# A fused Mamba and local-attention kernel: other group sizes, small steps moved from VectorE to GpSimd, joined VectorE operations, and products of zeros ahead of the first group's matmuls

## The chip, the cores and the metric

The kernel runs as one program on one core of a Trainium2 chip. The metric is device time in microseconds of that core. The time of a kernel is the median of its runs. Beside the timed runs there is one execution under the hardware profiler, and all rows below come from it.

## The reference, cut to what matters

The input is 16 sequences of 256 tokens with 128 features, all in float32. The work is a Mamba-like block, a transformer of two layers, and a normalisation after each of the two.

```python
# Mamba block, for x of shape (16, 256, 128)
u = silu(causal_conv4(x @ in_w + in_b))                    # 256 channels
delta = softplus((u @ dt1_w + dt1_b) @ dt2_w + dt2_b)
A = -exp(A_log)                                            # 16 states
h[t] = exp(delta*A) * h[t-1] + (exp(delta*A) - 1)/A * B * u   # a scan over 256 tokens
y = (sum_n C[n]*h[n] + D*u) * silu(x @ gate_w + gate_b)
x = layernorm(x + y @ out_w + out_b)
# two layers of local attention and a gated FFN
for l in 0, 1:
    q, k, v = split(shift_token(x) @ wqkv[l])              # 8 heads of 64
    q, k = rotary(l2norm(q)*qs), rotary(l2norm(k)*ks)      # windows of 64, own and previous
    x = x + softmax(8*q@k.T, masked) @ v @ wo[l]
    a, g = split(layernorm(shift_token(x)) @ w1[l] + b1[l])   # 341 hidden
    x = x + (a * gelu(g)) @ w2[l] + b2[l]
out = layernorm(x)
```

`shift_token` takes the second half of the features from the token before.

## The kernel before, in words

The sequences are cut into groups (`SIZES`). Before the change there are eight groups of two sequences, each 512 tokens or four tiles of 128. A group goes through the Mamba block on its own, then through attention and FFN of layer 0, then of layer 1. `QUAD` lists the (layer, group) pairs in the order in which attention and FFN take them, and `TILE` numbers the 64 (layer, group, tile) triples q = 0 to 63. Steps of Mamba take a group number `g`, steps of attention a tile number `q`, steps of the FFN a pair number `f`.

Each engine runs one written list of steps (`PE_ORDER`, `ACT_ORDER`, `DVE_ORDER`, `POOL_ORDER`, `SP_ORDER`). An engine never takes a later step first: when a step waits for a semaphore, all behind it on that engine waits too. So Mamba of group g+1, attention of layer 0 and of layer 1 are interleaved by the lists, not by the hardware.

- Mamba: `u_in` multiplies with `in_w` (TensorE), `convolve` makes the four-tap convolution (VectorE), `silu_u` and `silu_gate` follow (ScalarE), `rank` and `step_in` are the two small products for the step size, `softplus` is Abs, Exp and Ln on ScalarE, and `step_size` adds on VectorE. Then come 16 times one `decay` (ScalarE, Exp) and one `scan` (VectorE, all channels and sequences of the group in one instruction), whose result `state_y` sums on TensorE in the PSUM banks `Y`. `gated`, `mamba_out`, `mamba_sum` and `mamba_norm` end the block. All products of this block share the banks `Y`, so group g+1's `u_in` waits for group g's `gated`.
- Attention of a tile: `qk_in` and `v_in`; `squares` (ScalarE), `sums` (VectorE), `scale` (GpSimd, the power of -0.5) make the inverse norms `rn`; `rope` (VectorE) and `rotate` (GpSimd, for the keys) the rotation; `qk_T` transposes, `scores` multiplies; `row_max` (VectorE) takes the maximum and, before the change, also the product `nbias`; `softmax` (ScalarE) waits for `nbias`; then `probs_T`, `weighted`, `attended`, `out_T`.
- FFN of a pair: `attn_out`, `attn_sum`, `shift` (TensorE, the shifted half of the features), `ffn_stats`, `ffn_rstd` (GpSimd), `ffn_norm`, `norm_T`, `up_gate`, `gelus`, `up_a`, `hidden`, `down`, `ffn_sum`. All its products but the first two of `up_gate` pass through the one PSUM bank `M`.

A table of functions is loaded on ScalarE wherever the next function isn't in the table that is loaded (`ACT_TABLE_LOAD` in the profile). The diagonal matrices `diag` of `state_y` and the rotation tables are made at the start on GpSimd. Every matmul in float32 shows as two records in the trace.

Of the kernel before, what the change touches and what calls it, by code (L numbers as in the profile page):

```python
# [88 lines left out]
state_y 1 8, state_y 1 9, out_T 2, state_y 1 10, probs_T 3, state_y 1 11, weighted 3, state_y 1 12, out_T 3,
attn_out 0, state_y 1 13, state_y 1 14, state_y 1 15, shift 0, mamba_out 1, u_in 2, norm_T 0, layer_T 0 1,  # L90
up_gate 0, gate_in 2, qk_in 4, up_a 0 0, v_in 4, rank 2, qk_in 5, step_in 2, up_a 0 1, qk_T 4, up_a 0 2, qk_in 6,
v_in 5, scores 4, qk_in 7, down 0, qk_T 5, layer_T 1 0, probs_T 4, v_in 6, skip 2, scores 5, state_y 2 0,
state_y 2 1, weighted 4, state_y 2 2, state_y 2 3, probs_T 5, out_T 4, qk_T 6, v_in 7, scores 6, state_y 2 4,
weighted 5, state_y 2 5, qk_in 8, out_T 5, probs_T 6, v_in 8, state_y 2 6, qk_T 7, scores 7, qk_in 9,
state_y 2 7, weighted 6, state_y 2 8, out_T 6, probs_T 7, v_in 9, qk_T 8, state_y 2 9, weighted 7, scores 8,
out_T 7, qk_in 10, state_y 2 10, v_in 10, state_y 2 11, attn_out 1, probs_T 8, state_y 2 12, state_y 2 13,
qk_T 9, state_y 2 14, scores 9, qk_in 11, state_y 2 15, weighted 8, shift 1, mamba_out 2, probs_T 9, out_T 8,
u_in 3, qk_T 10, v_in 11, norm_T 1, scores 10, layer_T 0 2, gate_in 3, weighted 9, up_gate 1, probs_T 10,
up_a 1 0, qk_T 11, out_T 9, qk_in 12, scores 11, v_in 12, rank 3, weighted 10, up_a 1 1, qk_in 13, out_T 10,
probs_T 11, v_in 13, step_in 3, up_a 1 2, weighted 11, qk_T 12, qk_in 14, down 1, scores 12, layer_T 1 1,  # L100
out_T 11, qk_in 15, attn_out 2, qk_T 13, v_in 14, probs_T 12, shift 2, scores 13, skip 3, state_y 3 0,
weighted 12, out_T 12, norm_T 2, state_y 3 1, probs_T 13, v_in 15, state_y 3 2, qk_T 14, up_gate 2, weighted 13,
scores 14, state_y 3 3, up_a 2 0, state_y 3 4, out_T 13, up_a 2 1, qk_in 16, up_a 2 2, probs_T 14, state_y 3 5,
# [1426 lines left out]
```

## Time and profile before

| | us |
|---|---|
| median of 3 runs | 1129.08 (1127.99 to 1129.78) |
| the profiled execution's own time | 1122.38 |
| its span, first to last instruction | 1120.6 |
| TensorE busy with matmuls | 959.9 |
| VectorE busy | 917.7 |
| ScalarE busy | 821.5 |
| GpSimd busy | 479.2 |
| mean granted clock of TensorE | 0.943 of 2.4 GHz |

The span is what the rows cover; the execution's own time is 1.8 us longer. Busy time is a sum over stages that differ: the first 143 us and the last 110 us hold most of TensorE's idle time. The end of a matmul in the trace is modelled, so start-to-start distances say more than durations.

### The profile page before, as it was taken

The page shows a single profiled execution, that of the slowest core. Times are in us where ns is not written, and L with a number is a line of the kernel's source. Part 1 is how long each engine was busy: PE and PEld are TensorE (multiplying, and loading weights), DVE is VectorE, ACT ScalarE, POOL GpSimd, SP SyncE. Part 2 cuts the span into 40 slices and gives each one's busy share as a digit, 9 for nine tenths or more (in the row PEclk, how much of TensorE's full clock was granted, in tenths as well). Part 3 has the DMA queues.
Part 4 walks back from the last instruction along what each step waited for, and adds up shares of the span by engine and source line. Part 5 has one row for each costly group of instructions (what it writes and reads, how often), then busy time and mean ns, then how long its engine had stood idle before and what let it go on. Part 6 is the DMA issues. An engine that isn't in the chain of part 4 may idle for free. (4 is left out here: it accounts for less than half of the span.)

```text
span 1120.6 us, 26559 instructions
## 1 busy us (share of the span) xinstructions
PE 959.9 (86%) x10304; PEld 562.4 (50%) x10304; DVE 917.7 (82%) x1628; ACT 821.5 (73%) x1835; POOL 479.2 (43%) x308
## 2 busy tenths in 40 slices
PE   4466788789999999999989999999999899985865
PEld 1022443446464655556465556465555656753552
DVE  4787897899889998999889999999899966753822
ACT  3527765886998779886989689887997678772731
POOL 2704501653354444563345436535447354521701
PEclk8589888999999999999999999999999999998976
DMA  7000100100100001000000101010100001000100
GB/s 233 0 1 15 25 2 2 28 16 11 30 16 11 17 15 35 25 16 19 21 6 16 35 16 35 11 35 6 35 16 16 16 12 29 21 11 5 35 1 20
DMA packets 22000, 25.54 MB, mean 23 GB/s; under 512 B 2614, under 2 KB 13937, under 8 KB 21873
## 3 DMA queue, kind: packets, MB, share of 16 engines
q1 hardware_dynamic: 21873, 23.82, 8.1%
q8 instruction: 82, 1.34, 0.5%
q14 instruction: 45, 0.37, 0.1%
HBM read 9.13 MB, written 2.10 MB: 10 GB/s over the span
## 5 line engine op out<-in xcount | busy, mean ns | idle before, releaser
L718 POOL TENSOR_TENSOR rn<-ssc,expo 128x16 f32<-128x16 f32 x64 | 214.3, 3349 | 415.9 <-DVE ssc L1057 358.3
L993 DVE TENSOR_TENSOR_SCAN scan<-du,decay 128x1028 f32<-128x1028 f32 x128 | 292.6, 2319 | 1.8 <-ACT decay L804 1.8
L859 ACT ACTIVATE prob<-BB,nbias,rn 128x128 f32<-128x128 f32 x464 | 205.1, 465 | 26.9 <-DVE nbias L1100 25.6
L804 ACT ACTIVATE decay<-delta,negA 128x1024 f32<-128x1024 f32 x128 | 144.5, 1155 | 22.6 <-DVE scan L993 22.4
L1197 PE MATMUL YY<-scan,diag 64*64 64x512 f32 x1024 | 146.5, 658 | 16.7 <-DVE scan L993 16.4
L1197 PE MATMUL A<-wqkv,hT 128*128 128x512 f32 x256 | 125.1, 611 | 8.4 <-DVE ks L1076 5.9
L724 POOL TENSOR_TENSOR kr<-kc,ks 128x512 f32<-128x512 f32 x64 | 93.1, 1455 | 27.0 <-DVE ks L1076 25.4
L859 ACT ACTIVATION_READ_ACCUMULATOR prob<-BB,nbias,rn 128x1 f32 x464 | 98.8, 213 | 0.0
L1053 DVE TENSOR_REDUCE ss<-sq 128x16 f32<-128x1024 f32 x64 | 77.3, 1208 | 22.4 <-ACT sq L822 22.4
L822 ACT ACTIVATE sq<-A 128x512 f32<-128x512 f32 x128 | 72.3, 605 | 28.4 <-PE A L1197 25.9
L1096 DVE TENSOR_REDUCE nmax<-BB 128x4 f32<-128x512 f32 x116 | 74.4, 683 | 20.2 <-PE BB L1197 19.5
L1197 PEld LDWEIGHTS C<-v_even,probT 128*64 128x64 f32 x1024 | 65.8, 140 | 45.4 <-issue 40.1
L847 ACT ACTIVATE qkT<-BB 128x512 f32<-128x512 f32 x116 | 63.0, 598 | 32.3 <-PE BB L1349 32.0
L1197 PE MATMUL C<-v_even,probT 128*64 128x64 f32 x1024 | 74.5, 227 | 7.4 <-ACT v_odd L838 5.9
L1197 PE MATMUL M<-hnT,w 128*85 128x512 f32 (+1 forms) x128 | 70.4, 632 | 10.7 <-ACT hid L885 8.0
L828 ACT ACTIVATE probT<-BB 128x1024 f32<-128x1024 f32 x58 | 59.8, 1031 | 23.9 <-PE BB L1331 23.5
L1197 PE MATMUL C<-wqkv,hT 128*128 128x512 f32 x128 | 71.5, 640 | 6.7 <-ACT oT L869 3.2
L1197 PEld LDWEIGHTS A<-wqkv,hT 128*128 128x128 f32 x256 | 45.2, 191 | 61.9 <-issue 61.0
L1197 PE MATMUL C<-v_odd,probT 128*64 128x64 f32 x1024 | 74.9, 228 | 0.0
L727 POOL TENSOR_TENSOR kr<-kr,rn 128x512 f32<-128x512 f32 x64 | 71.0, 1109 | 5.0
L1197 PEld LDWEIGHTS M<-wo,oT 128*128 128x128 f32 x512 | 61.2, 198 | 14.3 <-ACT oT L869 7.9
L1197 PE MATMUL M<-wo,oT 128*128 128x128 f32 x512 | 63.4, 284 | 5.0 <-ACT oT L869 3.6
(159 smaller groups left out, 1942.7 us busy)
## 6 DMA issues: line engine op xcount, KB each, us to landing
v_even<-v_odd SPq DMA_DIRECT2D x96, 128.0 KB, 2.4
xT<-in_xT SPq DMA_DIRECT2D x8, 256.0 KB, 3.1
x<-in_x SPq DMA_DIRECT2D x8, 256.0 KB, 3.9
out<-outb SPq DMA_DIRECT2D x8, 256.0 KB, 2.4
wqkv<-in_wqkv SPq DMA_DIRECT2D x1, 1536.0 KB
w<-in_w SPq DMA_DIRECT2D x1, 682.0 KB
wo<-in_wo SPq DMA_DIRECT2D x1, 512.0 KB
bv<-in_bv SPq DMA_DIRECT2D x1, 328.0 KB
```

Of the source, the lines that this page charges most:

```text
L718: pool.tensor_tensor(rn[:, q % 2, :], ssc[:, :], expo[:, 0:2 * HEADS], ALU.pow).then_inc(rn_sb, 1)
L724: pool.tensor_tensor(kr[:, :], kc[:, :], ks[:, :], ALU.add).then_inc(rope_add, 1)
L727: pool.tensor_tensor(heads(kr[:, :]), heads(kr[:, :]), rn[:, q % 2, HEADS:].unsqueeze(2).to_broadcast((P, HEADS, DH)), ALU.mult).then_inc( ...
L804: act.activation(decay[:, at % A_RING, both(g), 1:], delta[:, both(g), :], ACT.Exp, scale=negA[:, n:n + 1]).then_inc(decay_sb, 1)
L822: act.activation(sq[:, a, :], A[a][:, :], ACT.Square).then_inc(sq_sb, 1)
L828: act.activation(probT[:, :, :, :].rearrange("p w h x -> p (w h x)"), pair(q)[:, :], ACT.Copy).then_inc(pT_sb, 1)
L847: act.activation(qkT[:, :, :, lo:lo + WIN], bank_of(q, r)[:, :].rearrange("p (a c x) -> p a c x", a=2, c=PAIRS), ACT.Copy).then_inc(qkT_sb, 1)
L859: ins = act.activation(prob[:, h, :], bank_of(q, a)[:, c * P:(c + 1) * P], ACT.Exp, bias=nbias[:, q % 2, h:h + 1], scale=rn[:, q % 2, h:h ...
L993: dve.tensor_tensor_scan(state, step, a, 0.0, ALU.add, ALU.mult).then_inc(scan_sb, 1)
L1053: dve.tensor_reduce(ss[:, :], sq[:, :, :].rearrange("p a (h x) -> p (a h) x", x=DH), AX.X, ALU.add).then_inc(ss_sb, 1)
L1096: dve.tensor_reduce(nmax[:, q % 2, a::2], bank_of(q, a)[:, :].rearrange("p (c x) -> p c x", x=P), AX.X, ALU.max, negate=True).then_inc(max ...
L1197: return pe.matmul(dst, lhsT, rhs, start=start, stop=stop, skip_group_check=True)
```

## The change

1. `SIZES` becomes ten groups: one sequence each in the first two and the last two, two in the six between. `QUAD` and all five lists are new. `part_a`, `part_b` and the rarely taken `scan_general` are cut to fit.
2. `softplus` loads one table that holds both Exp and Ln (set number 6). An Exp on a single element ahead of everything loads the first table.
3. From VectorE to GpSimd move the maximum with 1e-24 (`ssc`, now in `scale`), the product `nbias` (a step of its own, `exp_bias`) and the addition of eps in three norms (`rstd`).
4. VectorE's `rope` takes q and k in two operations in place of four, `row_max` both banks in one in place of two; `attended` loses its reciprocal to a step `inverse`, which the list puts earlier. Two more buffers let steps run ahead (`qkc`, `qks`, `rden`), and x3 has three in place of two.
5. `shift` also copies the unshifted half of the features into PSUM, by a product with the identity, so that `ffn_stats` and `ffn_norm` handle 128 columns at once.
6. At the start the loads are divided over SP's queue and ScalarE's, with semaphores of their own; `diag` is made by 2 GpSimd operations in place of 34; the rotation tables are made on VectorE.
7. `keep_busy(n)` issues n products of zeros (128x128 by 128 columns) on TensorE in the first group: 18 before `u_in`, 4 before `gate_in`, 14 before `rank`, 4 before `step_in`, 14 before `skip`.

```diff
-SIZES = (2, 2, 2, 2, 2, 2, 2, 2)
+SIZES = (1, 1, 2, 2, 2, 2, 2, 2, 1, 1)
+X3_RING = 3
...
+QUAD = [(0, 0), (0, 1), (0, 2), (1, 0), (1, 1), (0, 3), (1, 2), (0, 4), (1, 3), (0, 5), (1, 4), (0, 6), (1, 5),
+        (0, 7), (1, 6), (0, 8), (0, 9), (1, 7), (1, 8), (1, 9)]
...
 def scale(q):
+    pool.wait_ge(ss_sb, q + 1)
+    pool.tensor_scalar(ssc[:, :], ss[:, :], 1e-24, None, ALU.max).then_inc(ssc_sb, 1)
...
+def exp_bias(q):
+    pool.wait_ge(rn_sb, q + 1)
+    pool.wait_ge(max_sb, q + 1)
+    pool.tensor_tensor(nbias[:, q % 2, :], nmax[:, q % 2, :], rn[:, q % 2, 0:HEADS], ALU.mult).then_inc(nmax_sb, 1)
...
-def rstd(dst, ve, g, done):
+def rstd(dst, mv, ve, g, nth, aggr, var, done):
     n = tiles_of(g)
+    pool.wait_ge(aggr, nth)
+    pool.tensor_scalar(ve[:, 0:n], mv[:, 0:n, 1], EPS, None, ALU.add).then_inc(var, 1)
+    pool.wait_ge(var, nth)
     pool.tensor_tensor(dst[:, 0:n], ve[:, 0:n], expo[:, 0:n], ALU.pow).then_inc(done, 1)
...
-    for n in range(0, NST + 1):
-        ins = pool.tensor_scalar(diag[:, h, n, :], ident64[:, :], wsum[:, h, n:n + 1], None, ALU.mult)
+    ins = pool.tensor_tensor(diag[:, h], ident64[:, :].unsqueeze(1).to_broadcast(blocks),
+                             wsum[:, h, :].unsqueeze(2).to_broadcast(blocks), ALU.mult)
...
 def softplus(g):
+    load_table(EXP_AND_LN)
...
 def rope(q):
-    for a in range(2):
-        dve.tensor_tensor(heads(dst_c), heads(A[a][:, :]), cos, ALU.mult)
-        dve.tensor_tensor(dst_s..., swap, sin, ALU.mult).then_inc(rope_mul, 1)
+    dve.tensor_tensor(dst_c, src, cos, ALU.mult)
+    dve.tensor_tensor(dst_s, src[:, :, :, ::-1, :], sin, ALU.mult).then_inc(rope_mul, 2)
...
 def row_max(q):
-    for a in range(2):
-        dve.tensor_reduce(nmax[:, q % 2, a::2], bank_of(q, a)..., AX.X, ALU.max, negate=True).then_inc(max_sb, 1)
-    dve.tensor_tensor(nbias[:, q % 2, :], nmax[:, q % 2, :], rn[:, q % 2, 0:HEADS], ALU.mult).then_inc(nmax_sb, 1)
+    dve.tensor_reduce(nmax[:, q % 2, :]..., pair(q)..., AX.X, ALU.max, negate=True).then_inc(max_sb, 1)
...
 def ffn_stats(f):
     for i in range(tiles_of(g)):
-        dve.bn_stats(f_st[:, i, 0, :], x2[:, i, 0:D // 2])
-        ins = dve.bn_stats(f_st[:, i, 1, :], late[:, i, :])
+        ins = dve.bn_stats(f_st[:, i, :], rows[:, i, :])
...
+def keep_busy(n):
+    for _ in range(n):
+        mm(BB[:, 0:P], zeros[:, :], zeros[:, :])
...
 def shifted(f):
     for i in range(tiles_of(g)):
-        dst = M[:, i * D // 2:(i + 1) * D // 2]
-        ins = mm(dst, shift[:, :], x2[:, i, D // 2:], True, i % 2 == 0)
+        lo, mid, hi = i * D, i * D + D // 2, (i + 1) * D
+        mm(M[:, lo:mid], ident[:, :], x2[:, i, 0:D // 2])
+        ins = mm(M[:, mid:hi], shift[:, :], x2[:, i, D // 2:], True, i % 2 == 0)
```

In the new lists the first group's Mamba runs alone, then the second's; the first tile's `qk_in` stands between their products, but VectorE's list has no attention step until the second group's 16 scans are done (`gated 1, mamba_sum 1, sums 0, conv0 2, conv1 2, rope 0, ...`). The end of TensorE's list is `... weighted 63, up_a 18 0, up_a 18 1, out_T 63, up_a 18 2, down 18, attn_out 19, shift 19, norm_T 19, up_gate 19, up_a 19 0, up_a 19 1, up_a 19 2, down 19`; before it was `... weighted 63, out_T 63, attn_out 15, shift 15, ... down 15`.

## Rows read from the trace of the kernel before

**Rows 1.** The page: busy time, share of the span and instructions.
```profile
PE 959.9 (86%) x10304; PEld 562.4 (50%) x10304; DVE 917.7 (82%) x1628; ACT 821.5 (73%) x1835; POOL 479.2 (43%) x308
```

**Rows 2.** Stretches of the span: start:end, length, busy us by engine, clock, DMA.
```profile
0.00:36.00 36.00, 13.11 (x16) 3.44 (x16) 13.94 (x37) 15.05 (x17) 15.03 (x39) 0.74 0.55 181
36.00:76.00 40.00, 26.07 (x128) 4.25 (x128) 39.67 (x16) 17.20 (x16) 13.71 (x15) 0.68 0.00 1
76.00:110.00 34.00, 24.97 (x128) 11.75 (x128) 22.91 (x45) 19.82 (x27) 12.59 (x8) 0.90 0.04 13
...
143.00:950.00 807.00, 746.23 (x8352) 443.02 (x8350) 727.47 (x1281) 656.01 (x1479) 369.85 (x206) 0.99 0.08 19
...
1008.00:1079.00 71.00, 49.96 (x561) 32.29 (x560) 36.24 (x96) 37.53 (x100) 25.25 (x16) 0.90 0.07 16
1079.00:1121.00 42.00, 23.05 (x88) 16.20 (x86) 10.99 (x45) 4.49 (x6) 5.53 (x5) 0.70 0.05 13
```

**Rows 3.** Waits of TensorE from 143 to 950 us, those that VectorE ended: total, times, longest.
```profile
PE C L1394 <- DVE o_s L1088: 6.2, 7, 2.5
...
PE M L1423 <- DVE hn L1141: 5.1, 5, 2.3
...
PE A L1197 <- DVE ks L1076: 3.9, 5, 2.2
...
PE YY L1197 <- DVE scan L993: 3.4, 4, 1.3
```

**Rows 4.** Groups by line: operands, shapes, count, busy us, mean ns, idle before.
```profile
L993 DVE TENSOR_TENSOR_SCAN scan<-du,decay 128x1028 f32<-128x1028 f32 x128 | 292.6, 2319 | 1.8 <-ACT decay L804 1.8
...
L1141 DVE TENSOR_SCALAR hn<-M,f_mv,f_rs 128x64 f32<-128x64 f32 x64 | 21.6, 338 | 0.0
...
L885 ACT ACT_TABLE_LOAD x16 | 20.5, 1283 | 6.8 <-PE A L1197 6.6
...
L1197 PE MATMUL M<-x,shift 128*128 128x64 f32 x128 | 20.1, 280 | 0.9 <-DVE x L1113 0.9
...
L1057 DVE TENSOR_SCALAR ssc<-ss 128x16 f32<-128x16 f32 x64 | 16.8, 262 | 4.5 <-POOL rn L718 2.4
...
L1123 DVE BATCH_NORM_STATS2 f_st<-M 128x6 f32<-128x64 f32 x64 | 13.8, 215 | 0.3 <-issue 0.3
...
L1100 DVE TENSOR_TENSOR nbias<-nmax,rn 128x8 f32<-128x8 f32 x64 | 12.6, 197 | 6.7
```

**Rows 5.** Timeline of the start: start us, us, engine, line, operation, what ended the idle.
```profile
2.40 1.76 DVE L910 MEMSET v_even<- 128x2048 f32 x1 [0.38 <-issue]
...
6.04 3.78 PE L1197 MATMUL YY<-xT,in_w 128*128 128x512 f32 x4 [6.04 <-DMA gate_w<-in_gate_w]
...
11.96 1.98 PE L1197 MATMUL YY<-xT,gate_w 128*128 128x512 f32 x4 [2.14 <-ACT upre L762]
...
27.63 1.28 ACT L793 ACT_TABLE_LOAD   x1
28.92 1.06 ACT L793 ACTIVATE th<-th 128x1024 f32<-128x1024 f32 x1
...
36.29 39.67 DVE L993 TENSOR_TENSOR_SCAN scan<-du,decay 128x1028 f32<-128x1028 f32 x16 [1.48 <-ACT decay L804]
```

**Rows 6.** Timeline of TensorE in the last FFN.
```profile
1080.48 6.34 PE L1197 MATMUL M<-wo,oT 128*128 128x128 f32 x32 [0.69 <-ACT oT L869]
...
1096.44 3.43 PE L1197 MATMUL A<-hnT,w 128*128 128x512 f32 x4 [0.96 <-ACT hnT L876]
...
1108.13 5.27 PE L1197 MATMUL M<-w,hid 128*128 128x128 f32 x24 [0.93 <-DVE hid L1150]
```

**Rows 7.** Timeline of GpSimd's power and VectorE's scans around 342 us.
```profile
341.79 4.83 POOL L718 TENSOR_TENSOR rn<-ssc,expo 128x16 f32<-128x16 f32 x1 [1.99 <-DVE ssc L1057]
...
395.76 2.91 POOL L718 TENSOR_TENSOR rn<-ssc,expo 128x16 f32<-128x16 f32 x1 [15.38 <-DVE ssc L1057]
...
341.62 6.68 DVE L993 TENSOR_TENSOR_SCAN scan<-du,decay 128x1028 f32<-128x1028 f32 x3
```

More of the change, by code:

```diff
@@ L89 @@
[L89 to L103, printed above, removed]
@@ L159 @@
-probs_T 63, weighted 63, out_T 63, attn_out 15, shift 15, norm_T 15, up_gate 15, up_a 15 0, up_a 15 1, up_a 15 2,
-down 15"""
+state_y 0 13, state_y 0 14, state_y 0 15, mamba_out 0, u_in 1, gate_in 1, rank 1, step_in 1, layer_T 0 0,
+qk_in 0, v_in 0, skip 1, state_y 1 0, state_y 1 1, state_y 1 2, state_y 1 3, state_y 1 4, v_in 1, state_y 1 5,
+state_y 1 6, state_y 1 7, state_y 1 8, state_y 1 9, state_y 1 10, state_y 1 11, state_y 1 12, state_y 1 13,
+state_y 1 14, state_y 1 15, mamba_out 1, u_in 2, gate_in 2, rank 2, qk_in 1, layer_T 0 1, step_in 2, qk_T 0,
@@ new lines @@
+state_y 3 9, qk_T 8, layer_T 1 1, weighted 7, scores 8, state_y 3 10, qk_in 10, out_T 7, state_y 3 11,
+attn_out 2, v_in 10, state_y 3 12, probs_T 8, state_y 3 13, qk_T 9, weighted 8, state_y 3 14, scores 9,
+state_y 3 15, shift 2, qk_in 11, mamba_out 3, out_T 8, probs_T 9, u_in 4, qk_T 10, norm_T 2, v_in 11, scores 10,
+layer_T 0 3, gate_in 4, weighted 9, up_gate 2, probs_T 10, out_T 9, up_a 2 0, qk_T 11, qk_in 12, up_a 2 1,
+scores 11, v_in 12, rank 4, weighted 10, up_a 2 2, qk_in 13, out_T 10, probs_T 11, step_in 4, down 2, qk_in 14,
@@ new lines @@
+qk_T 32, state_y 6 10, v_in 33, scores 32, out_T 31, state_y 6 11, attn_out 9, v_in 34, probs_T 32, state_y 6 12,
+state_y 6 13, qk_T 33, weighted 32, state_y 6 14, scores 33, shift 9, out_T 32, state_y 6 15, qk_in 35,
+mamba_out 6, probs_T 33, v_in 35, norm_T 9, qk_T 34, u_in 7, scores 34, layer_T 0 6, gate_in 7, weighted 33,
+up_gate 9, probs_T 34, qk_in 36, qk_T 35, up_a 9 0, out_T 33, scores 35, v_in 36, up_a 9 1, rank 7, weighted 34,
+qk_in 37, out_T 34, up_a 9 2, probs_T 35, v_in 37, step_in 7, weighted 35, qk_T 36, qk_in 38, down 9, scores 36,
@@ new lines @@
+out_T 39, state_y 7 11, v_in 42, attn_out 11, probs_T 40, state_y 7 12, qk_T 41, weighted 40, state_y 7 13,
+scores 41, state_y 7 14, state_y 7 15, shift 11, qk_in 43, mamba_out 7, probs_T 41, out_T 40, qk_T 42, u_in 8,
+norm_T 11, scores 42, layer_T 0 7, v_in 43, gate_in 8, up_gate 11, weighted 41, rank 8, probs_T 42, out_T 41,
+step_in 8, up_a 11 0, qk_T 43, up_a 11 1, qk_in 44, scores 43, skip 8, v_in 44, up_a 11 2, weighted 42,
+state_y 8 0, qk_in 45, probs_T 43, state_y 8 1, down 11, out_T 42, qk_T 44, v_in 45, state_y 8 2, qk_in 46,
@@ L162 @@
 ACT_ORDER = """
[L163 removed]
+u_in 0, silu_u 0, silu_gate 0, rank 0, softplus 0, decay 0 0, decay 0 1, decay 0 2, decay 0 3, decay 0 4,
 decay 0 5, decay 0 6, decay 0 7, decay 0 8, decay 0 9, decay 0 10, decay 0 11, decay 0 12, decay 0 13,
[L165 to L166 removed]
```

682 lines of the change are left out of this document (368 added, 314 removed).

## The prediction

> **What bounds the kernel now.** I read the busy shares first: TensorE is the fullest with 959.9 of 1120.6 us, VectorE second with 917.7, GpSimd holds only 43% [rows 1]. Then the stretches [rows 2]. From 143 to 950 us TensorE is busy for 746.2 of 807 us and VectorE for 727.5: the reader is to see that this stretch is bound by TensorE's work, with VectorE close behind, and that only 60.8 us of TensorE idle time are there to be won. The ends are different. Up to 110 us TensorE is busy for 64 us, mostly at a clock of 0.68 to 0.74; the last 42 us hold 23 us of it at 0.70. There a chain of dependent steps sets the time. Last I read the waits of the middle stretch: of those that TensorE's matmuls spend, VectorE ended 18.6 us in the four largest [rows 3], most others ScalarE.
>
> **Start, groups of one sequence.** Before, the first scan starts at 36.3 us and the 16 scans take 39.7 [rows 5], 76.0 together. After, four things change up to the first scan.
> - Table loads: five stand in the first 36 us, at 1.28 each [rows 5]. The first is made while the weights arrive, those ahead of Ln and of the first decay go: 3 x 1.28 = 3.8 us less.
> - Widths are halved. TensorE's 13.1 us, ScalarE's 15.1 less its 6.4 of loads, and VectorE's 13.9 less some 7 of memsets and coefficients make 29 us [rows 2]; I estimate 20 of them on the chain, and that half the width saves 0.4 of these (a fixed part stays): 8 us.
> - The 18 products of zeros are issued once VectorE's memsets are done, at 4.2 us [rows 5], and `u_in` stands behind them, where it started at 6.0. They are 36 records. Wide-apart bounds for one record of 128 columns: 6.34/32 = 0.20 us in the last `attn_out` at the low clock [rows 6], and half of it at the other level. So they take 3.6 to 7.1 us and `u_in` starts at 8 to 11. Its own four records took 3.78 us for 512 columns, `gate_in`'s took 1.98 [rows 5]: 256 columns at the faster rate are 1.0. `u_in` ends near 10.5 in place of 9.8: a loss of 0.7 us. What the zeros buy is the rate for `rank` and `step_in`, some 1 us each, counted in the 0.4 above.
> - The rotation tables on VectorE, 12 small operations of about 0.2 us (the smallest in its groups are 0.20 to 0.26 [rows 4]), are in front of `step_size`: 2.5 us, of which I count 0.5, since `step_size` waits for ScalarE meanwhile.
>
> Sum: 3.8 + 8 - 0.7 - 0.5 = 10.6; first scan near 25.5. A scan of 514 columns is about half of 2.32 us [rows 4], from start to start 1.15, 16 of them 18.5, up to 44. Then the second sequence needs its own chain from `gated` to the first scan. The stretch 76 to 110 us is that chain at full width, 34 us with 11 us of attention work on VectorE in it [rows 2]; at half width, without that work and one load in place of three, I take 16. With its scans: 44 + 16 + 18.5 = 78.5. So both kernels have two sequences through the scan at nearly the same time, 76.0 against 78.5: what the short first group wins, the additional serial chain gives back. The next chain is full width in both, with two loads fewer (2.6 us), and in it tiles 0 to 2 already have `rope` and `sums` (before: 0 and 1). With that and an FFN that can start after two tiles, I put the start at **-5 us**, between +3 (nothing of the head start is used) and -15 (the FFN of two tiles fills TensorE's idle 34 us of 143).
>
> **Middle.** Three terms.
> - TensorE gets 64 products more, one a tile and layer, in `shift`. The 64 shift products of the same size are 128 records and 20.1 us [rows 4]: between 14 (records overlap in the trace) and 20 us in all, 12 of 14 in the middle. **+12 us**, since this engine is the bound.
> - VectorE loses: `ssc` 16.8, `nbias` 12.6 [rows 4]; half the statistics, 64 operations of 0.215 against a slightly longer one of 128 columns, 10; half of `ffn_norm` likewise (0.338 each), 13; the joined `rope` and `row_max`, where each join saves only the fixed part, 12; the eps additions, 9. That is 73. Added are 64 half scans for 32 whole ones, 80 us at an estimated 1.25 each (half of 2.32 and a fixed bit) for 74, and small steps of two more groups, together 8. Net -65 of 917.7, 7%. It is worth what TensorE waits for VectorE: I take the four rows of 18.6 and some shorter ones as gone, **-20 us**. Bounds: 0, if the next waits take their place, and -40, if two thirds of the idle time go.
> - ScalarE: taken by the written order, loads are 58 before (16 of them for Gelu [rows 4]) and 55 after: one in place of three per `softplus`, but two more groups and four more FFN pairs. 3 x 1.28 = 4 us less, and 64 half decays for 32 whole ones cost that again. 0, bounds -5 to +5. The Trainium skill (ScalarE: Activation LUTs, What ACT_TABLE_LOAD costs) gives a switch as 1.28 us plus 1.38 us of drain. In this trace the load ends at 28.91 and the next activation starts at 28.92 [rows 5], with no such gap; by the page three loads were 8 us, by the row 4.
>
> Middle: **-8 us**.
>
> **End.** The last FFN, four tiles, follows the last attention alone: 42 us, TensorE at 0.70 [rows 2]. After, it has two tiles, and the FFN of the other two is for the most part issued among tiles 62 and 63. Halves of what is shown: `attn_out` 6.34, `up_gate` 3.43, `down` 5.27 save 7.5 [rows 6]; the third chunk of `up_gate`, `up_a` and `hidden` 3; statistics, norm, additions and copies on VectorE and ScalarE 4. That is 14.5. Against it, `up_a 18 2` and `down 18` with `hidden` and `ffn_sum` stand between `out_T 63` and `attn_out 19`, and all use bank M: 4.5. Net **-10 us**, bounds 0 (FFN 18 isn't covered) and -18 (the clock stays up, too). The FFN before tiles 60 to 63 stays four tiles long, as does its gap.
>
> **Sum.** -5 - 8 - 10 = -23, from the profiled execution's 1122.4 to 1099.4. The median of the runs shown is 6.7 above that execution; I carry that over: **1106 us**.
>
> **The moved steps, and what speaks against them.** `nbias` was 0.2 us on VectorE right behind `row_max`. On GpSimd it is queued with powers and rotations, and `softmax` waits for it, as `probs_T` on TensorE does for that. The power took 2.91 us alone and 4.83 where it met three scans in a row [rows 7]: GpSimd does not get on while VectorE scans. A GpSimd step that starts under a scan thus waits for its end, up to 2.3 us for one. By the row every `exp_bias` met by a scan is late by about 1.2 us in the mean, plus what is queued before it. The Trainium skill says the same rule (GPSIMD Engine Reference, Key points): GpSimd shares its SBUF interfaces with VectorE and meets contention from VectorE instructions with two SBUF inputs, which the scan is. By that rule the step gets slower exactly where scans are dense; by the busy sums alone it would be free. The trace agrees with the rule. I count its price at 0 because the lists put other work between `row_max` and `softmax`, and keep it as a rival.
>
> **Rivals.**
> 1. GpSimd becomes the late one: some 30 of the 50 tiles that run beside scans lose 1.5 us each between `row_max` and `softmax`, +45, less a third that other work covers: +30, with the +12 for the identity products and nothing won in the middle. +42 - 15 = +27: 1156; at half the price 1141. It decides once the mean delay exceeds some 1 us a tile. For: the rows on the power. Against: GpSimd is idle for 57%, and TensorE now waits hardly at all for `softmax`. I take 1142.
> 2. VectorE was the true pace-maker: its lead of 65 us shows in TensorE's idle time down to 20 of 61, the FFN of two tiles fills the start: -15 - 28 - 14 = -57 at best, typically -42: 1087.
> 3. TensorE's added work eats it: middle +8, start 0, end -8: 1129, no change.
> 4. The change doesn't do what it says at the start: the zeros delay `u_in` and the clock falls before the scans anyway. That costs 3 to 5 us on the forecast, and stays inside its own range: 1110.
>
> **How the numbers follow.** Forecast (with 4) 0.47, rival 2 0.29, rival 3 0.08, rival 1 0.16. The measurement tells 0.2% (2.3 us) from no change. Faster: 0.47 + 0.29 less a tail, plus some of rival 3, is 0.77; the same 0.05; slower 0.18. The bounds of the terms, -15 to +3, -28 to +12 and -18 to 0, reach from -61 to +15; the range takes in rival 2 and the near half of rival 1: 1075 to 1137. The likeliest case alone is 1097 to 1115.
>
> **What would show it.** First scan at 24 to 27 us and the first scan of the third group at 104 to 110. `shift` rows with 64 more products. In the middle TensorE's idle share under 6% of the stretch, its busy time higher by some 12 us, VectorE's total near 855. 55 table loads. The end from the last `attn_out` about 10 us shorter. Wrong, if ScalarE's waits for `nbias`, now ended by GpSimd, exceed 60 us, if the second group's scans start after 68 us, or if TensorE's idle time in the middle doesn't fall.

## The result, and the profile after

The changed kernel takes 1113.93 us in the median (1111.94 to 1118.06), against 1128.53 for the kernel before on the same chip: a ratio of 0.9876 with a 95% interval of 0.9845 to 0.9908, or 14 us faster. Forecast were 1106, range 1075 to 1137. The profiled executions differ by less: 1122.38 us before, 1113.69 after, so 8.7 us. The execution of before that was profiled lay below its median, the one of after on it. So of the 23 us that the terms added up to, the traces show 8.7 and the timed runs 14.

The page of the kernel after, busy time by engine (answers to [rows 1]):

```profile
PE 977.8 (88%) x10892; PEld 607.1 (55%) x10892; DVE 866.8 (78%) x1249; ACT 832.2 (75%) x1909; POOL 560.3 (50%) x448
```

Its stretches, columns as in [rows 2]:

```profile
0.00:36.00 36.00, 25.32 (x172) 19.39 (x172) 24.48 (x59) 14.39 (x23) 5.58 (x9) 0.91 0.52 167
36.00:76.00 40.00, 25.63 (x190) 10.49 (x194) 28.46 (x40) 22.70 (x37) 1.64 (x3) 0.83 0.04 11
76.00:110.00 34.00, 23.17 (x132) 8.16 (x132) 26.33 (x35) 16.86 (x24) 13.10 (x10) 0.90 0.04 8
143.00:950.00 807.00, 754.73 (x8674) 467.83 (x8674) 685.49 (x939) 663.88 (x1536) 454.64 (x349) 0.99 0.08 19
1008.00:1070.00 62.00, 48.34 (x498) 31.44 (x499) 28.08 (x51) 31.20 (x82) 27.46 (x26) 0.89 0.08 18
1070.00:1112.00 42.00, 25.01 (x174) 17.72 (x173) 12.50 (x44) 11.30 (x29) 6.83 (x13) 0.72 0.05 13
```

The reader is to see two columns. TensorE is busy for 977.8 us, 17.9 more than before, in a shorter span; VectorE for 866.8, 50.9 less. TensorE's idle time (span less busy) fell by 26.6 us, and 17.9 of these went to a longer busy time: without the records of the products of zeros it would be 962.7 us, so they alone are 15.1 of the 17.9. From 143 to 950 us the idle time went from 60.8 to 52.3. In a window of fixed length the busy time must rise by the same 8.5, and the work in the window is not the same in both kernels, so this row doesn't tell what the stretch won. The milestones below do.

Waits of TensorE's matmuls in that stretch (total, times, longest), beside [rows 3]:

```profile
PE BB L1406 <- ACT prob L918: 17.7, 13, 6.3
PE BB L1424 <- POOL kr L775: 4.2, 1, 4.2
PE AA L1254 <- DVE qks L1141: 3.4, 2, 2.6
...
PE YY L1254 <- DVE scan L1066: 2.7, 3, 1.1
```

The VectorE rows that headed the list are gone or smaller, as forecast. At the head stands `prob`, ScalarE's softmax; over the whole span this wait was 4.9 us before and is 18.4 now. (`BB`, `AA` and `YY` are PSUM banks of the products that wait.)

Groups by line of the kernel after, columns as in [rows 4]:

```profile
L1066 DVE TENSOR_TENSOR_SCAN scan<-du,decay 128x1028 f32<-128x1028 f32 x96 | 218.5, 2302 | 6.9 <-ACT decay L863 6.9
...
L1066 DVE TENSOR_TENSOR_SCAN scan<-du,decay 128x514 f32<-128x514 f32 x64 | 75.0, 1221 | 9.1 <-PE YY L1254 7.8 <-ACT decay L863 1.0 <-DVE du L1038 0.2
L754 POOL TENSOR_SCALAR ssc<-ss 128x16 f32<-128x16 f32 x64 | 49.4, 772 | 166.8 <-DVE ss L1123 165.9
...
L766 POOL TENSOR_TENSOR nbias<-nmax,rn 128x8 f32<-128x8 f32 x64 | 30.5, 477 | 178.1 <-DVE nmax L1161 178.0
...
L1254 PE MATMUL M<-x,ident 128*128 128x64 f32 x128 | 25.1, 277 | 1.8 <-DVE x L1176 1.8
...
L1254 PE MATMUL M<-x,shift 128*128 128x64 f32 x128 | 24.7, 275 | 0.0
...
L1254 PE MATMUL BB<-zeros 128*128 128x128 f32 x108 | 16.0, 314 | 4.4 <-DVE v_even L970 4.4
...
L1184 DVE BATCH_NORM_STATS2 f_st<-M 128x6 f32<-128x128 f32 x64 | 14.6, 285 | 16.6 <-PE M L1254 16.6
```

The identity products overlap with the shift products, so their sum in the group is no cost of its own. The scans cost the same 293.5 us in 160 instructions as in 128. The two small steps grew on their way to GpSimd: `ssc` from 262 ns to 772, `nbias` from 197 to 477. These means mix two kinds. Of the 64 `nbias`, the 56 that meet no scan take 205 ns, hardly more than on VectorE. The 7 that start while VectorE scans take 1753 ns in the mean and 2282 at most, and each ends with that scan (220.23 to 222.26 us, the scan until 222.27). One starts at 367.04, 0.15 us ahead of three scans in a row, and ends with the third: 6.8 us. For `ssc` it is 46 at 313 ns and 17 at 1956.

### The profile page after: what moved, and what is told of

The parts are those of the page before. It is cut to its first block, busy times and chain, and to the rows that moved or that the text cites. A ratio compares the mean times of both kernels' runs of the same rounds, so it can differ in the third digit from the quotient of the medians.

```text
span 1111.9 us, 27668 instructions
## 1 busy us (share of the span) xinstructions
PE 977.8 (88%) x10892; PEld 607.1 (55%) x10892; DVE 866.8 (78%) x1249; ACT 832.2 (75%) x1909; POOL 560.3 (50%) x448
## 4 chain that ended last, share of the span: by engine, by line
PE 53%; ACT 13%; issue 8%; DVE 6%; POOL 5%; POOLq 0%; ACTq 0%; DVEq 0%
PE M L1254 14%; PE AA L1254 9%; PE YY L1254 9%; PE C L1254 7%; ACT prob L918 7%; PE BB L1254 4%; PE BB L1418 3%; PE BB L1406 2%; DVE scan L1066 2%; DVE nmax L1161 2%; PE C L1469 1%; ACT hid L944 1%; POOL nbias L766 1%; PE BB L1424 1%; POOL rn L759 1%
## 5 line engine op out<-in xcount | busy, mean ns | idle before, releaser
L1066 DVE TENSOR_TENSOR_SCAN scan<-du,decay 128x1028 f32<-128x1028 f32 (+1 forms) x160 | 293.5, 1870 | 16.0 <-ACT decay L863 7.9
L918 ACT ACTIVATE prob<-BB,nbias,rn 128x128 f32<-128x128 f32 x472 | 208.8, 463 | 44.3 <-POOL nbias L766 43.9
L863 ACT ACTIVATE decay<-delta,negA 128x1024 f32<-128x1024 f32 (+1 forms) x160 | 153.5, 985 | 15.3 <-DVE scan L1066 10.4
L1254 PE MATMUL YY<-scan,diag 64*64 64x512 f32 (+1 forms) x1280 | 139.7, 530 | 14.6 <-DVE scan L1066 14.6
L1254 PE MATMUL AA<-wqkv,hT 128*128 128x512 f32 x256 | 131.2, 636 | 15.3 <-DVE qks L1141 11.4
L772 POOL TENSOR_TENSOR kr<-qkc,qks 128x512 f32<-128x512 f32 x64 | 89.5, 1398 | 7.7 <-DVE qks L1141 6.3
L881 ACT ACTIVATE sq<-AA 128x512 f32<-128x512 f32 x128 | 72.3, 607 | 24.7 <-PE AA L1254 24.3
L1161 DVE TENSOR_REDUCE nmax<-BB 128x8 f32<-128x1024 f32 x59 | 71.7, 1216 | 24.2 <-PE BB L1254 24.1
L1140 DVE TENSOR_TENSOR qkc<-AA,rope_c 128x1024 f32<-128x1024 f32 x64 | 77.6, 1212 | 13.7 <-PE AA L1254 8.5
L1254 PEld LDWEIGHTS C<-v_even,probT 128*64 128x64 f32 x1024 | 65.5, 139 | 32.5 <-issue 27.4
L1254 PE MATMUL M<-hnT,w 128*128 128x512 f32 (+3 forms) x160 | 75.4, 555 | 8.1 <-DVE hid L1207 4.2
L1141 DVE TENSOR_TENSOR qks<-AA,rope_s 128x1024 f32<-128x1024 f32 x64 | 77.6, 1212 | 0.0
L887 ACT ACTIVATE probT<-BB 128x1024 f32<-128x1024 f32 x59 | 60.8, 1030 | 19.4 <-PE BB L1406 18.8
```

What stands on the lines that cost most here:

```text
L772: pool.tensor_tensor(kr[:, :], qkc[:, q % 2, 1, :], qks[:, q % 2, 1, :], ALU.add).then_inc(rope_add, 1)
L863: act.activation(decay[:, at % A_RING, both(g), 1:], delta[:, both(g), :], ACT.Exp, scale=negA[:, n:n + 1]).then_inc(decay_sb, 1)
L881: act.activation(sq[:, a, :], A[a][:, :], ACT.Square).then_inc(sq_sb, 1)
L918: ins = act.activation(prob[:, h, :], bank_of(q, a)[:, c * P:(c + 1) * P], ACT.Exp, bias=nbias[:, q % 2, h:h + 1], scale=rn[:, q % 2, h:h ...
L1066: dve.tensor_tensor_scan(state, step, a, 0.0, ALU.add, ALU.mult).then_inc(scan_sb, 1)
L1140: dve.tensor_tensor(dst_c, src, cos, ALU.mult)
```

## Where the time went, by milestones

Start in us of the first scan, of the `gated` that ends Mamba for four sequences, and of VectorE's `o_s` (step `attended`) for single tiles. The kernels of the last three columns are in the next section.

| | before | after | after, no zeros | old groups, no zeros | old groups, single last ones |
|---|---|---|---|---|---|
| first scan | 36.3 | 29.2 | 25.3 | 29.8 | 29.9 |
| `gated` for 4 sequences | 167.3 | 166.0 | 161.5 | 155.0 | 155.4 |
| tile 0 | 127.9 | 130.1 | 125.6 | 117.0 | 117.4 |
| tile 16 | 398.3 | 392.3 | 388.4 | 380.9 | 381.3 |
| tile 40 | 763.3 | 745.2 | 745.5 | 744.3 | 743.1 |
| tile 44 | 824.9 | 822.8 | 822.0 | 805.7 | 818.3 |
| tile 63 | 1077.9 | 1079.5 | 1077.2 | 1058.4 | 1074.8 |
| end of span | 1120.6 | 1111.9 | 1109.8 | 1099.2 | 1104.4 |

After against before, the lead is 1.3 us at four sequences, 18.1 at tile 40, 2.1 at tile 44, -1.5 at tile 63, and the 8.7 of the result are made behind tile 63 (42.7 us before, 32.5 after). So the middle does win 17 us, and loses 16 of them in the 80 us in which the first of the two last groups has its scans.

**The start.** TensorE, ScalarE (from its table load) and VectorE of the kernel after up to the first scan, columns as in [rows 5]:

```profile
4.36 7.07 PE L1254 MATMUL BB<-zeros 128*128 128x128 f32 x36 [4.36 <-DVE v_even L970]
11.27 1.03 PE L1254 MATMUL YY<-xT,in_w 128*128 128x256 f32 x4
12.13 1.05 PE L1254 MATMUL BB<-zeros 128*128 128x128 f32 x8
13.03 1.09 PE L1254 MATMUL YY<-xT,gate_w 128*128 128x256 f32 x4
13.96 3.29 PE L1254 MATMUL BB<-zeros 128*128 128x128 f32 x28
```

```profile
19.97 1.28 ACT L823 ACT_TABLE_LOAD   x1
...
22.71 0.63 ACT L854 ACTIVATE th<-th 128x512 f32<-128x512 f32 x1
```

```profile
21.19 2.23 DVE L1006 CAST mask<-prob 128x512 bf16<-128x512 f32 x1
23.34 2.10 DVE L1013 TENSOR_TENSOR rope_c<-rope_c,bv 128x128 f32<-128x128 f32 x1
...
25.63 0.28 DVE L1013 TENSOR_TENSOR rope_c<-rope_c,bv 128x128 f32<-128x128 f32 x1
...
27.05 0.74 DVE L1045 SCALAR_TENSOR_TENSOR delta<-YY,th 128x256 f32<-128x256 f32 x2
...
29.16 2.35 DVE L1066 TENSOR_TENSOR_SCAN scan<-du,decay 128x514 f32<-128x514 f32 x2 [0.77 <-ACT decay L863]
...
64.96 3.47 DVE L1066 TENSOR_TENSOR_SCAN scan<-du,decay 128x514 f32<-128x514 f32 x3 [0.25 <-DVE du L1038]
```

GpSimd in the same stretch:

```profile
21.07 4.23 POOL L732 TENSOR_TENSOR diag<-ident,wsum 128x1088 f32<-128x1088 f32 x2 [7.41 <-DVEq L1000]
```

The zeros' 36 records take 7.07 us, the upper bound of the forecast, and `u_in` starts at 11.3. ScalarE has its Ln done at 23.3, but `step_size` (`delta`) starts at 27.05: VectorE is still at the mask and the tables. That is 3.7 us where I had counted 0.5. The list in front of `step_size` takes 6.0 us, from 21.05 to 27.05, where the forecast had 2.5 for the tables and nothing for the mask, whose cast stood at 94.9 us before the change and took 0.42 there.

**The end.** TensorE's products of the last FFN, beside [rows 6]:

```profile
1086.40 2.02 PE L1254 MATMUL M<-wo,oT 128*128 128x128 f32 x16 [0.61 <-DVE outb L1223]
...
1094.57 2.05 PE L1254 MATMUL AA<-hnT,w 128*128 128x256 f32 x4 [0.75 <-ACT hnT L935]
...
1103.44 2.90 PE L1254 MATMUL M<-w,hid 128*128 128x128 f32 x12 [0.67 <-DVE hid L1207]
```

Together 7.0 us in place of 15.0: 8.1 less, where I had 7.5.

## The experiments

All ratios are to the kernel before in the same set of runs. It was at 1128.5 us beside the change and at 1123.5 beside the last four, so kernels of different sets are compared by ratio; 0.1% is 1.1 us.

| kernel | median us | ratio | 95% interval |
|---|---|---|---|
| the change | 1113.9 | 0.9876 | 0.9845 to 0.9908 |
| no zeros | 1109.0 | 0.9843 | 0.9814 to 0.9872 |
| `nbias` on VectorE | 1121.2 | 0.9957 | 0.9935 to 0.9979 |
| no identity product | 1116.2 | 0.9907 | 0.9876 to 0.9938 |
| old groups and lists | 1102.2 | 0.9791 | 0.9763 to 0.9819 |
| ... and no zeros | 1101.2 | 0.9779 | 0.9749 to 0.9809 |
| ... and tables later | 1102.7 | 0.9777 | 0.9745 to 0.9809 |
| old groups, `nbias` on GpSimd | 1185.1 | 1.0526 | 1.0494 to 1.0559 |
| old groups, no identity product | 1100.2 | 0.9769 | 0.9740 to 0.9798 |
| old start, single last groups | 1108.4 | 0.9871 | 0.9843 to 0.9899 |
| new start, old last groups | 1106.2 | 0.9833 | 0.9808 to 0.9857 |
| old groups, max and eps on VectorE | 1107.7 | 0.9845 | 0.9820 to 0.9870 |
| old groups, `rope` and `row_max` parted | 1105.0 | 0.9828 | 0.9803 to 0.9854 |

### The zeros

```diff
 def keep_busy(n):
-    for _ in range(n):
-        mm(BB[:, 0:P], zeros[:, :], zeros[:, :])
+    return
```

> The changed kernel (1113.9 us) without any product of zeros; nothing else is different. Theory A, by which the zeros buy the faster rate for the first group's products: the products of rank and step_in go from about 1.0 to 2 us each, u_in starts at 5 to 6 us in place of 11.3 but its products take 2 us in place of 1.0; first scan at 27 to 30 us (29.2 with zeros), end within 2 us of 1114. Theory B, by which the zeros only stand in front of u_in: first scan 4 us earlier (25) and the end 3 to 4 us earlier, 1110. What VectorE does between the last coefficient and step_size (21.0 to 27.0 us in the trace of the changed kernel) would hide part of either.

Measured 1109.0 us, 5 less than with them (0.9843 against 0.9876; the intervals overlap, so the gain in time isn't resolved). The first scan comes at 25.3 us, where theory B had it. TensorE and VectorE without the zeros:

```profile
4.36 2.08 PE L1254 MATMUL YY<-xT,in_w 128*128 128x256 f32 x4 [4.36 <-DVE v_even L970]
```

```profile
23.20 0.74 DVE L1045 SCALAR_TENSOR_TENSOR delta<-YY,th 128x256 f32<-128x256 f32 x2
...
25.32 2.35 DVE L1066 TENSOR_TENSOR_SCAN scan<-du,decay 128x514 f32<-128x514 f32 x2 [0.77 <-ACT decay L863]
```

`u_in` takes 2.08 us in place of 1.03 but starts 6.9 earlier. The zeros do halve each of the four products, and on `step_in` they shorten ScalarE's part: Ln is done at 20.8 without and 23.3 with them, 2.5 apart where `upre` was 3.4 apart. But `delta` waits for VectorE's own list, which began when `upre` came, so the whole delay stays: 3.8 us at the first scan, 4.3 at the second `gated`, 4.5 at the third.

The table shows this lead at tile 16 and no more at tile 40. It was lost in one place. TensorE in the same four-microsecond steps behind the same work, first without zeros, then the change:

```profile
492.00:496.00 4.00, 3.75 (x32) 3.56 (x32) 3.76 (x4) 0.34 (x1) 3.92 (x4) 1.00 0.00 0
496.00:500.00 4.00, 0.65 (x17) 0.59 (x17) 3.81 (x3) 4.00 (x17) 2.99 (x3) 1.00 0.01 2
500.00:504.00 4.00, 4.00 (x17) 3.16 (x15) 2.30 (x1) 1.84 (x3) 2.87 (x1) 0.55 0.00 0
504.00:508.00 4.00, 4.00 (x47) 3.76 (x48) 0.00 (x0) 0.60 (x2) 0.00 (x0) 0.50 0.02 4
508.00:512.00 4.00, 4.00 (x72) 3.09 (x72) 0.67 (x1) 0.49 (x2) 0.00 (x0) 0.67 0.00 0
```

```profile
500.00:504.00 4.00, 0.49 (x16) 0.50 (x16) 3.98 (x3) 4.00 (x17) 3.07 (x2) 1.00 0.01 2
504.00:508.00 4.00, 4.00 (x50) 3.39 (x46) 2.30 (x1) 1.91 (x3) 2.95 (x2) 1.00 0.00 0
508.00:512.00 4.00, 3.85 (x96) 2.71 (x96) 0.96 (x1) 1.09 (x2) 0.00 (x0) 1.00 0.02 4
```

Both stand still for some 3.5 us while they wait for `prob`. In one the granted clock then drops to 0.50, in the other it stays at 1.00. Between the two `gated` that surround it, the same 1393 records took 125.35 and 120.65 us: 4.7 us, all of the lead. So in this pair of traces the lead isn't used up by the schedule, but lost to the clock in one of two single executions. The timed medians lie 5 us apart, which fits but is not resolved. With the old groups (below) the first scans lie 3.5 us apart, too, 33.3 and 29.8, but tile 4 only 0.8 us, and the times agree.

### `nbias` and the identity product, in the new lists

```diff
 def row_max(q):
+    dve.wait_ge(rn_sb, q + 1)
+    dve.wait_ge(max_sb, q + 1)
+    dve.tensor_tensor(nbias[...], nmax[...], rn[...], ALU.mult).then_inc(nmax_sb, 1)
 ...
 def exp_bias(q):
-    pool.tensor_tensor(nbias[...], nmax[...], rn[...], ALU.mult).then_inc(nmax_sb, 1)
+    pass
```

> The changed kernel with the product nbias back on VectorE, directly behind the joined row_max; ssc and the eps additions stay on GpSimd. If the step on GpSimd is late (the rival of the prediction): ScalarE's waits for nbias fall from 44 us to 25 to 30, TensorE's waits for softmax in the middle from 18 to 5, and the time falls by 5 to 15 us, to 1100 to 1109. If the relief of VectorE is worth more than the delay (the forecast): VectorE's busy time rises by 12 us and the time by 0 to 5 us, to 1114 to 1119.

Measured 0.9957, 7 to 9 us slower than the change (the intervals don't meet). In these lists the move to GpSimd pays, and more than the 0 to 5 us expected: VectorE's busy time is 27.8 us higher (894.6), where 12 were expected, since `nbias` takes 327 ns here and the scans some 6 us more. It pays although the step is later on GpSimd: ScalarE waits for it for 28.8 us before the change, 35.6 in this kernel and 44.3 in the change, and TensorE for `prob` for 7.6 us here and 18.4 there.

```diff
 def shifted(f):
-        mm(M[:, lo:mid], ident[:, :], x2[:, i, 0:D // 2])
 def ffn_stats(f):
+        dve.bn_stats(f_st[:, i, 0, :], x2[:, i, 0:D // 2])
+        ins = dve.bn_stats(f_st[:, i, 1, :], late[:, i, :])
 ...
```

> The changed kernel with shift, ffn_stats and ffn_norm as before: no product with the identity, statistics and normalisation in halves of 64 columns. If TensorE's work is the bound in the middle: 64 products less are 12 to 14 us less on TensorE, and VectorE's 20 us more hide in its idle time: 1102 to 1108. If VectorE and TensorE are equally short there: within 3 us of 1114. If VectorE is what counts: 1116 to 1122.

Measured 0.9907 against 0.9876, overlapping. TensorE has 11.0 us less work (966.8), VectorE 24.2 more (891.0), and no difference in time is resolved: the two cancel, or nearly.

### The step edits without the new groups

```diff
-SIZES = (1, 1, 2, 2, 2, 2, 2, 2, 1, 1)
+SIZES = (2, 2, 2, 2, 2, 2, 2, 2)
```

The five lists are those of before; `inverse` stands right ahead of `attended`, `nbias` is on VectorE.

> All changes to the steps themselves, but eight groups of two sequences with the lists of before (inverse put directly ahead of attended) and nbias on VectorE behind row_max. To be held against the changed kernel with nbias on VectorE: the rest between them is the group sizes and the new lists. If the single sequences bring the gain, at the end above all: 1120 to 1128, that is near the kernel before. If the edits to the steps bring it: 1108 to 1116. My forecast put 10 us to the end, 5 to the start and 8 to the steps: 1118 to 1122.

Measured 0.9791, 1102.2 us, outside all that was expected: the step edits alone win 24 us, and the new sizes and lists take 10 of them away (19 with `nbias` in the same place). Its first scan comes at 33.3 us, later than after's 29.2, yet four sequences are through at 155.9 us, 10 earlier. VectorE is busier than in the change (878.2 us against 866.8), but ScalarE is busy for 805.8 against 832.2, with 47 table loads against 55.

> The kernel of e4 (steps edited, eight groups of two with the lists of before, nbias on VectorE, 1102.2 us) without the products of zeros. In e4 u_in starts behind 18 of them. If they are a loss in this start too, as e1 suggests (1109.0 without, 1113.9 with): first scan earlier by 1 to 4 us and 1098 to 1101. If they pay for full-width products (rank and step_in of 512 columns are twice as long): 1103 to 1107.

Measured 0.9779: no difference from the run with zeros.

```diff
 def gated(g):
     ...
+    if g == 0:
+        masks()
+        rotation_tables()
```

> As e5, and the mask and the rotation tables are made on VectorE after the first group's gated, where it waits for mamba_out, in place of ahead of step_size 0. In the changed kernel these stood from 21.05 to 27.05 us with Ln done at 23.3, so 3.7 us of them were on the path, most of it in two operations of 2.1 to 2.2 us that ran while GpSimd made diag. If that is the path: first scan 2 to 4 us earlier than in e5 and the time 2 to 4 us less. If diag on GpSimd is the next thing late, or the tables delay the second group's convolution by as much: within 1.5 us of e5.

Measured 0.9777, again no difference. The first scan did not come earlier but later, 31.2 us against 29.8. In the kernel just above, with two sequences in the first group and the tables ahead of `step_size`, Ln ends at 26.7 us, when VectorE's tables are done, so they delay nothing; here Ln ends at 28.5, since `step_in` took 3.78 us in place of 1.98. So the run does not price the tables in the first group of one sequence. What it shows is what the two long operations take elsewhere. VectorE:

```profile
69.88 0.42 DVE L963 CAST mask<-prob 128x512 bf16<-128x512 f32 x1
70.22 0.28 DVE L970 TENSOR_TENSOR rope_c<-rope_c,bv 128x128 f32<-128x128 f32 x1
```

The same two operations took 2.23 and 2.10 us in the change, where GpSimd's two `diag` products ran from 21.07 to 25.30. So in the change some 3.6 us of VectorE's list at the start are two engines in each other's way. What their absence would bring to the first scan of that kernel was not run.

### The first rival's mechanism

```diff
 def exp_bias(q):
-    pass
+    ...
+    pool.wait_ge(rn_sb, q + 1)
+    pool.wait_ge(max_sb, q + 1)
+    pool.tensor_tensor(nbias[...], nmax[...], rn[...], ALU.mult).then_inc(nmax_sb, 1)
 ...
 def row_max(q):
-    dve.wait_ge(rn_sb, q + 1)
-    dve.wait_ge(max_sb, q + 1)
-    dve.tensor_tensor(nbias[...], nmax[...], rn[...], ALU.mult).then_inc(nmax_sb, 1)
```

GpSimd's list of before gets the 64 steps `exp_bias` (`... scale 2, rotate 2, exp_bias 1, scale 3, rotate 3, exp_bias 2, ...`).

> The kernel of e4 with nbias on GpSimd as in the changed kernel, put into the list of before at the latest place that the other steps' order allows. In the new lists nbias on VectorE cost 7 us (e2 1121.2, changed 1113.9). Theory R, that the list was laid out for one place of the step and any move costs: here the move to GpSimd costs, 1104 to 1112. Theory F, that VectorE's relief is worth it wherever it is: 1096 to 1101. ScalarE's waits for nbias were 32 us in e4 and 44 in the changed kernel.

Measured 1.0526, 1185 us, far beyond both theories: 83 us slower than the same kernel with `nbias` on VectorE. Waits of this kernel, then of the change:

```profile
ACT prob L861 <- POOL nbias L709: 95.4, 42, 5.5
...
PE BB L1349 <- ACT prob L861: 52.8, 25, 5.8
```

```profile
ACT prob L918 <- POOL nbias L766: 44.3, 29, 6.9
...
PE BB L1406 <- ACT prob L918: 18.4, 14, 6.3
```

Mean duration is 699 ns here and 477 in the change: 17 of the 64 start under a scan here, with 2063 ns in the mean, and 7 there; those that meet no scan take 205 in both. From the end of `row_max` to the end of `nbias` it is 1.90 us in the mean here and 0.37 with `nbias` on VectorE; in the change it is 0.87, and 0.30 before it. Rival 1 was a real mechanism with the size I gave it and more, and its limit of some 1 us a tile lies between the two kernels; what kept it away is where the new lists put this step. How much of the 83 us is this step's own delay and how much my choice of its places in a list not made for it, this run can't part.

```diff
 def shifted(f):
-        mm(M[:, lo:mid], ident[:, :], x2[:, i, 0:D // 2])
```

> The kernel of e4 without the product with the identity, statistics and normalisation in halves as before. In the new lists this cost 2.3 us (e3 1116.2 against 1113.9). If TensorE's 14 to 20 us less count for more here: 1097 to 1100. If as in e3, VectorE's time counts at least as much: 1102 to 1107.

Measured 0.9769 against 0.9791, overlapping, though 1100.2 us is the fastest median of all. TensorE has 7.7 us less work and 5.0 more idle time in its trace.

### Which end loses

The lists are spliced at `gated` of the sequences 13 and 14, with tile 42 next: old lists up to there and new ones behind it, or the reverse.

```diff
-SIZES = (2, 2, 2, 2, 2, 2, 2, 2)
+SIZES = (2, 2, 2, 2, 2, 2, 2, 1, 1)
```

> Groups of two sequences with the lists of before up to tile 42, then the last two groups of one sequence with the new lists; nbias on VectorE, no products of zeros. It differs from the kernel with the old groups and no zeros (1101.2 us) only behind tile 42. Theory L (the single last groups lose where their chains run one after the other): in the changed kernel tiles 40 to 44 took 77.6 us against 61.4 with the old groups, and what is behind tile 63 took 32.5 against 40.7, so it loses some 18 us before tile 63 and wins 8 behind it: 1108 to 1113 us. Rival E (the shorter end is a clean gain, and the loss before it is GpSimd's late nbias or the rest of the new lists): 1090 to 1094 us.

Measured 0.9871 against 0.9779 with pairs: the intervals don't meet, and 1108.4 us lies where theory L had it. Rival E's clean gain is out, and so is a late `nbias` on GpSimd, which this kernel hasn't got. The order of the new lists is not: single groups and their lists come together here. VectorE's `o_s` of tiles 40 and 44 with pairs, then with single last groups:

```profile
744.30 0.69 DVE L1111 TENSOR_TENSOR o_s<-C,rden 128x512 f32<-128x512 f32 x1
...
805.67 0.69 DVE L1111 TENSOR_TENSOR o_s<-C,rden 128x512 f32<-128x512 f32 x1
```

```profile
743.06 0.69 DVE L1127 TENSOR_TENSOR o_s<-C,rden 128x512 f32<-128x512 f32 x1
...
818.33 0.69 DVE L1127 TENSOR_TENSOR o_s<-C,rden 128x512 f32<-128x512 f32 x1
```

Between tiles 40 and 44 this ending loses 13.9 us; from tile 40 to 63 it loses 17.6, and behind tile 63 it wins 11.2 (29.6 us in place of 40.8): 6.4 lost. The stretch 744 to 806 us shows a part of how, first pairs, then single groups:

```profile
744.00:806.00 62.00, 59.02 (x648) 38.02 (x646) 52.11 (x103) 52.45 (x119) 33.98 (x28) 1.00 0.07 19
```

```profile
744.00:806.00 62.00, 53.17 (x555) 33.79 (x555) 46.98 (x87) 46.12 (x112) 31.32 (x24) 0.97 0.07 16
```

All four engines do less in it: TensorE stands idle for 8.8 us in place of 3.0. One wait of 4.2 us for GpSimd's `kr` is there in both kernels with this list; what makes up the rest of the distance, no run shows.

```diff
-SIZES = (1, 1, 2, 2, 2, 2, 2, 2, 1, 1)
+SIZES = (1, 1, 2, 2, 2, 2, 2, 2, 2)
```

> The complement: the changed kernel without zeros up to tile 42 (single sequences in the first two groups, nbias on GpSimd), then the old lists with a last group of two sequences, nbias on VectorE from there. The changed kernel without zeros was at 1109 us. Theory L: the loss of 18 us before tile 63 goes, the end gets 8 longer: 1098 to 1101 us. Rival E: the end gets 8 to 10 longer and nothing comes back: 1117 to 1119 us.

Measured 0.9833 against 0.9843 without the edit, no resolved difference, and between the two theories: theory L had 1098 to 1101 us. In the traces, from tile 40 to 63 it takes 320.2 us in place of 331.7, and behind tile 63 42.2 in place of 32.6, so that what is won in front is nearly all paid behind. At tile 40 it stands at 743.8 us and the old groups at 744.3: so in these traces two first groups of one sequence are worth nothing there. Behind tile 40 it is 7.5 us slower than they, part of which may be the seam.

### What the step edits win with

```diff
 def sums(q):
+    dve.tensor_scalar(ssc[:, :], ss[:, :], 1e-24, None, ALU.max).then_inc(ssc_sb, 1)
 ...
 def stats(...):
+    dve.tensor_scalar(ve[...], mv[..., 1], EPS, None, ALU.add).then_inc(var, 1)
 ...
```

> All step edits with the old groups (1102.2 us), but the maximum with 1e-24 and the addition of eps are VectorE's again, 64 and 24 small operations of 0.2 to 0.26 us plus their waits. Theory V (VectorE's relief is what the step edits win): some 20 of 39 us of what VectorE was relieved of in these lists come back, and the time rises by 8 to 12 us, to 1110 to 1114. Rival J (the gain sits in the joined operations and the removed table loads): within 3 us of 1102.

Measured 0.9845 against 0.9791, 6 us slower; VectorE's busy time rose by 20.1 us. Less than theory V had, and past rival J's bound.

```diff
 def rope(q):
-    dve.tensor_tensor(dst_c, src, cos, ALU.mult)
+    for a in range(2):
+        dve.tensor_tensor(dst_c[:, a], src[:, a], cos[:, a], ALU.mult)
 ...
```

> All step edits with the old groups (1102.2 us), but rope is four operations and the row maximum two again. Theory J (the joined operations carry the gain): the time rises by 8 to 12 us, to 1110 to 1114. Rival V: VectorE gets 10 to 15 us of fixed parts back, of which a third reaches the end, 1104 to 1107; a rival beside it: the parted operations can start on the first half earlier, and the time falls by 2 us or more.

Measured 0.9828 against 0.9791, overlapping, 4 us at best; VectorE 12.3 us busier. The size that rival V gave for it. By the ratios both runs give one rate: of each us taken from VectorE 0.30 and 0.34 reach the end, the second of them not resolved.

This explains about half of the 24 us. VectorE is busy for 39.5 us less than before in the kernel with the old groups, and at 0.30 that is 12 us, an estimate from these runs. No run takes back the rest by itself: it has 47 table loads in place of 58 and ScalarE is busy for 15.7 us less, and its first scan comes 3 us earlier.

## Why the prediction was right, and where not

- **First scan near 25.5 us: 29.2.** The step that failed is the zeros' net loss of 0.7 and the tables' 0.5, with the mask left out. Without zeros the first scan comes at 25.3. I added up TensorE's chain and let `step_size` wait for ScalarE; it waits for VectorE, whose chain from `upre` on doesn't get shorter when TensorE gets faster.
- **Two sequences done at 78.5: 85.7.** 4.1 of it from the first group, 0.9 more in the second chain (16.9 us, forecast 16), 2.2 in its scans, which stop once for 1.72 us. The scans of the second group start at 65.0, inside the bound of 68, and the first scan of the third at 116.3, outside 104 to 110. So the start term of -5 is -1.3 by four sequences. That the serial second chain gives the head start back was foreseen; that nothing of it is left shows in tile 40 of the last experiments.
- **TensorE +12 in the middle.** Taking the identity products out takes 11.0 us off TensorE's busy time over the whole span, where I had 14 to 20. They cost nothing that the time shows, in either set of lists; that VectorE's relief balances them fits, but no run has the one without the other. TensorE's idle time from 143 to 950 us did fall, to 52.3 us or 6.5% of the stretch; the forecast had under 6%.
- **VectorE's relief of 65 us worth 20: 50.9 us.** The forecast's own terms add up to 59, not 65: 73 less 6 for the scans and 8 for the small steps. The rate of 0.31 held (0.30 and, not resolved, 0.34 where parts are undone in the old lists). The size was off because neighbours overlap: the busy times of VectorE's groups by line add up to 984.3 us before and 910.6 after, 73.7 less, and its busy time as a whole fell by 50.9 (855 forecast, 866.8 found). An instruction taken out gives back less than the duration that its row shows.
- **ScalarE 0.** The 55 table loads are as forecast, 1283 ns each, and behind the load at 19.97 the next activation starts at 21.26, with no gap. But ScalarE's busy time rose by 10.7 us. The 64 half decays take 46.4 us in place of 37.0 for 32 whole ones, 9.4 more where I had 4, and the groups of one keep 8 loads that the old groups don't have (55 against 47). What the 26 us of ScalarE between these two kernels are worth, no run shows.
- **End -10: -10.2** from tile 63 to the last instruction. But I priced it only behind tile 63 and never asked what two short groups do to the stretch in front. That is the largest miss: 11 and 18 us before tile 63 by the two spliced kernels, so that the single last groups with their lists bring no gain there but a loss of 2 and 6 us in the traces. The middle's -8 fell with it: it was 17 us ahead at tile 40, yet the lead of 1.3 us at four sequences is -1.5 at tile 63.
- **The carry-over of 6.7 us.** It belongs to before's profiled execution and not to the change; the profiled execution of after is its median. Without it the terms gave 1099.4 for a profiled time of 1113.7. That the median came within 8 us owes half to this term, which is luck: the forecast of 1106 holds with its start, middle and end at -1.3, +2.8 and -10.2 in the traces, where it had -5, -8 and -10.
- **Rival 1.** Its test, 60 us of ScalarE's waits for `nbias`, reads 44.3, and the mean delay from `row_max` to `nbias` is 0.87 us, under the 1 us that it needed. I had taken some 30 tiles as hit by a scan; 8 are, 7 at 1.75 us in the mean and one at 6.8. The Trainium skill (GPSIMD Engine Reference, Key points) names the contention and gives no size for it there; the trace agrees with the rule, with 205 ns away from the scans and up to 2282 for those that start under one.
- **Rivals 2 and 3.** TensorE's idle time in the middle is 52.3 us and not 20, and the kernel is 18 us ahead at tile 40, so neither a free run of VectorE's lead nor a loss to TensorE's added work shows.
- **Rival 4** holds: the zeros cost 3.8 us at the first scan, as priced, and 5 in the median, not resolved. The clock did fall ahead of the scans: it is granted at 0.62 from 28 to 36 us, with the drop to the lower level at 27.3 us, behind an idle stretch in which TensorE waits for `delta`, and the first scan starts at 29.16. Over the first 36 us it reads 0.91, and 0.74 before.

Open: what part of the 14 us between tiles 40 and 44 is the group of one sequence itself and what the order of the lists around it; and what of the 10 to 19 us that sizes and lists cost is ScalarE's added work. Every kernel with the old groups, all step edits and `nbias` on VectorE is faster than the change and than the kernel before. The fastest median, 1100.2 us, is the one without the identity products; one with neither zeros nor identity products was not run.
